# Forming the feed-forward weights inside the last attention output product, and a different split of the mixer's element-wise work between VectorE, ScalarE and GpSimd

## The chip, the cores and the metric

One core of a Trainium2 chip runs one program. The metric is the device time of that core in microseconds, the median of several runs. The core has a matrix engine (TensorE, in the rows PE, with PEld for its weight loads), VectorE (DVE), ScalarE (ACT), GpSimd (POOL) and a queue engine (SyncE, SP) that issues nearly all transfers. Each engine works through its own instruction list in order; semaphores join them.

## The reference, cut to what matters

`x` has 8 sequences of 512 positions and 1024 features. Four layers follow each other, each with a residual and a layer norm in front:

```
x = x + attention(layernorm(x))          # per sequence
x = x + ffn(layernorm(x))                # kind 1 in the kernel
x = x + mixer(layernorm(x))              # kind 2; mixes over the 8 sequences ("l") per position
x = x + ffn(layernorm(x))                # kind 3, the same weights as kind 1
ffn(x):   base = x @ W_base.T + b_base
          decoded_e = (x @ enc.T) @ (coefs_e * mask_e).T      # rank 40, three experts e
          return base + 0.5 * sum_e real_inverse_fourier(decoded_e)
mixer(x): x + up(xmid + gated two-layer state-space block(gelu(down(x))))
```

Everything in `ffn` behind `x` is linear, so the kernel forms one 1024 x 1024 weight `W = W_base.T + 0.5 * enc.T @ basis` with `basis = (sum of masked coefs).T @ inverse transform`. In the mixer each position's 8 x 8 causal weights over `l` are laid out as 128 x 128 matrices `cb`: entries ahead of a position, behind it, and ones on the diagonal.

## The kernel before, in words

**Attention program.** Tokens are handled in 8 sequences (`BATCH`) of 8 head groups each, one group per step `M` of a hand-written pipeline. The output product of a sequence comes in two runs of four token tiles (`output(b, run)`): each tile is 8 chunks of three float32r products (high x high, low x high, high x low), 24 matmuls of 512 columns, and VectorE adds it to the residual (`add_residual`, L718) before SyncE stores it in the DRAM array `x1` (L372). Products of float32 operands that are split into a float32r high part and a remainder stand for full precision throughout.

**Weights of the feed-forward layer.** The class `Setup` (`early`) holds buffers that lie in the same place in both programs. When the last AV product is done, SyncE loads the coefficients, masks, four pairs of rows of the inverse transform (`dft_pairs`), `enc` and the first two pairs of rows of `W_base` (L82 to L88). VectorE forms the masked sum (`mix_coefs`, L101 to L106). Behind the last output run TensorE computes `basis` in full float32, 16 products of 512 columns (L114); VectorE copies it to SBUF (L124); the program ends, and SyncE first waits for all of `x1`.

**Mixer program.** Work goes in 8 blocks of four token tiles; a tile is 16 positions of all 8 sequences, loaded by one transfer of 512 KB. The list `ORDER` is the hand-written order of stages for one turn of the loop, and each engine runs its part of each stage in that order. A stage belongs to an event `(kind, tile)`: `moments` (VectorE statistics L1329, L1331; GpSimd's inverse root L1177, L1179), `norm` (VectorE L1339), `turn` (8 TensorE transposes L1559, ScalarE's high part L1246, VectorE's low part L1346, GpSimd's `post`), `gemm` (24 matmuls per half L1564 to L1566), `add` (L1354). `down`, `h_...`, `up` are the mixer's own stages; `h_mix` (L1680) is the product with the 128 x 128 matrices.

Before the first turn stands a `head`: `weights`, then norm and turn of tiles (1,0) and (1,1). In `weights` TensorE forms the 8 row blocks of `enc.T @ basis` in full float32 (L1711, 16 products), VectorE adds each to `W_base` (L1516), ScalarE rounds the sum to float32r (L1303), VectorE forms the remainder (L1504). SyncE in the meantime issues the first two x tiles (L1146), the down weights (L1154), 17 parameters (L1156) and 7 constants (L1159), waits for six of the remainders, and loads six more x tiles (L1146): some x tiles lie where rows of `W_base` were. `post` of the first tile waits for all 24 parameters and constants (`late_in`).

`post(e)` on GpSimd, for kind 1 and 3, adds the bias to the residual in four pieces (L1193). For kind 2 the residual is the normed input as well, so it first adds `xn` in four pieces (L1189), then the bias in four. GpSimd handles `post` of tile (2,3) ahead of the inverse root of (3,0), as the order has it, and `norm(e)` waits for `post(e-2)`.

`h_weight` builds `cb`: VectorE multiplies the product in PSUM by a mask for one side (L1423), by the mask for the other side (L1425), copies an edge of the identity (L1427), adds the sides (L1429) and adds the identity (L1431); then it forms the step weights (L1436 to L1446). `h_mix` multiplies both (L1455) and TensorE takes the result (L1680).

Of the kernel before, what the change touches and what calls it, by code (L numbers as in the profile page):

```python
# [5 lines left out]
P = 128  # L6
# [7 lines left out]
U8 = mybir.dt.uint8  # L14
PENDING = []
# [7 lines left out]
class Setup:  # L23
# [5 lines left out]
    DMA = 16  # L29

    def __init__(self, nc, ctx, w, c):
# [7 lines left out]
        self.tok = self.place("tok", [P, 3, self.TILES, 256])  # L39
        self.mixer = self.place("mixer", [P, self.TILES, 4, P])  # L40
        self.h_mid = self.place("h_mid", [P, 2, self.COLS])
        self.mask = self.place("mask", [P, self.CH, experts, rank], U8)
        self.wsum = self.place("wsum", [P, self.CH, rank])
        self.ident = self.place("ident", [P, P])
        self.experts = experts
# [3 lines left out]
        self.enc = self.mixer[0:rank, 2:4, :, :].rearrange("p a b c -> p (a b c)")  # L49
        self.basis = self.h_mid[0:rank, :, :].rearrange("p a b -> p (a b)")  # L50
# [9 lines left out]
        self.basis_part, self.basis_ready, self.basis_done = sem("basis_part"), sem("basis_ready"), sem("basis_done")  # L60
# [19 lines left out]
    def load(self, sp):  # L80
# [5 lines left out]
        sp.dma_start(self.enc, self.w["enc"]).then_inc(self.params_in, self.DMA)  # L86
        for k in range(2):
            sp.dma_start(self.base_pairs[k], self.rows(self.w["base_t"], k)).then_inc(self.base_in, self.DMA)  # L88

    def load_rest(self, sp):  # L90
        for k in range(2, self.CH // 2):
            if k < self.CH // 2 - 1:
                sp.wait_ge(self.basis_part, k + 1)
            else:
                sp.wait_ge(self.basis_ready, 2)
            sp.dma_start(self.base_pairs[k], self.rows(self.w["base_t"], k)).then_inc(self.pair_in[k], self.DMA)

    def mix_coefs(self, dve):
# [5 lines left out]
        for n in range(2, self.experts):  # L104
            dve.wait_ge(self.wsum_step, n)
            nc.vector.tensor_tensor(wsum[:, :, :], wsum[:, :, :], coef[:, :, n, :], ALU.add).then_inc(self.wsum_step, 1)  # L106

    def basis_product(self, pe, banks):
        pe.wait_ge(self.wsum_step, self.experts)
        for n in range(self.CH):  # L110
            if n % 2 == 0:
                pe.wait_ge(self.pair_in[n // 2], self.DMA)
            for h in range(2):
                mm = self.nc.tensor.matmul(banks[0:self.RANK, h, :], self.wsum[:, n, :], self.dft(n)[:, h * self.COLS:(h + 1) * self.COLS],  # L114
                                           start=(n == 0), stop=(n == self.CH - 1))
                if n == self.CH - 1:
                    mm.then_inc(self.basis_ready, 1)
                elif n % 2 and h:
                    mm.then_inc(self.basis_part, 1)
        pe.wait_ge(self.params_in, 2 * self.DMA)  # L120

    def basis_out(self, dve, banks):
        dve.wait_ge(self.basis_ready, 2)
# [1716 lines left out]
```

## Time and profile before

| | us |
|---|---|
| median of 3 runs | 2946.47 (2938.45 to 2946.77) |
| the profiled execution's own time | 2937.39 |
| its span, first to last instruction | 2935.6 |
| TensorE busy | 2706.6 (92%) |
| VectorE busy | 1676.3 (57%) |
| ScalarE busy | 1151.1 (39%) |
| GpSimd busy | 947.0 (32%) |

A row of a timeline has the start and length of an instruction (or of several equal ones), its engine, line, and what it writes and reads; in brackets how long the engine stood idle ahead of it, and what ended that. Times in the trace are microseconds from the span's start. The attention part ends and the mixer part begins between 1640 and 1700 us; below this stretch is called the seam. A turn of the mixer's loop takes about 147 us, and there are 8.

### The profile page before, as it was taken

The page shows a single profiled execution, that of the slowest core. Times are in us where ns is not written, and L with a number is a line of the kernel's source. Part 1 is how long each engine was busy: PE and PEld are TensorE (multiplying, and loading weights), DVE is VectorE, ACT ScalarE, POOL GpSimd, SP SyncE. Part 2 cuts the span into 40 slices and gives each one's busy share as a digit, 9 for nine tenths or more (in the row PEclk, how much of TensorE's full clock was granted, in tenths as well). Part 3 has the DMA queues.
Part 4 walks back from the last instruction along what each step waited for, and adds up shares of the span by engine and source line. Part 5 has one row for each costly group of instructions (what it writes and reads, how often), then busy time and mean ns, then how long its engine had stood idle before and what let it go on. Part 6 is the DMA issues. An engine that isn't in the chain of part 4 may idle for free. (4 is left out here: it accounts for less than half of the span.)

```text
span 2935.6 us, 41188 instructions
## 1 busy us (share of the span) xinstructions
PE 2706.6 (92%) x14784; PEld 1961.1 (67%) x14784; DVE 1676.3 (57%) x4305; ACT 1151.1 (39%) x2509; POOL 947.0 (32%) x1460
## 2 busy tenths in 40 slices
PE   5888999999999999999999987999999999999988
PEld 3555666657566676575665566777777777777766
DVE  3563564663745646636444346666666666666653
ACT  3763464562644645626455013222222222222220
POOL 2333122221231122212313044444444444444412
PEclk8999999999999999999999888999999999999989
DMA  5764554454536455544455410010101010101001
GB/s 159 209 169 151 176 125 143 126 115 145 126 91 172 124 140 130 113 150 120 107 146 172 145 43 1 7 52 7 52 6 53 6 53 5 54 5 54 5 26 29
DMA packets 103628, 272.24 MB, mean 93 GB/s; under 512 B 12122, under 2 KB 23514, under 8 KB 101122
## 3 DMA queue, kind: packets, MB, share of 16 engines
q1 hardware_dynamic: 102706, 269.55, 34.0%
q8 instruction: 118, 1.93, 0.3%
q14 instruction: 84, 0.69, 0.1%
q10 hardware_dynamic: 720, 0.07, 0.0%
HBM read 168.40 MB, written 50.33 MB: 75 GB/s over the span
## 5 line engine op out<-in xcount | busy, mean ns | idle before, releaser
L668 DVE CUSTOM_DVE_ANT_0 ps_attn<-ps_attn,later_keys 128x512 f32<-128x512 f32 (+3 forms) x1024 | 488.1, 508 | 392.8 <-PE ps_attn L841 392.3
L474 POOL TENSOR_SCALAR_AFFINE_SELECT pt<-pt 128x512 f32<-128x512 f32 x256 | 163.4, 649 | 868.1 <-ACT pt L561 868.1
L1564 PE MATMUL ps_mixer<-m_w_hi,m_xt_hi 128*128 128x512 f32 x1024 | 418.2, 408 | 1.6 <-DVE m_xt_lo L1346 1.6
L561 ACT ACTIVATE pt<-ps_attn 128x512 f32<-128x512 f32 (+1 forms) x704 | 380.4, 558 | 82.8 <-PE ps_attn L868 75.8
L1566 PE MATMUL ps_mixer<-m_w_lo,m_xt_hi 128*128 128x512 f32 x1024 | 400.6, 391 | 0.0
L1565 PE MATMUL ps_mixer<-m_w_hi,m_xt_lo 128*128 128x512 f32 x1024 | 400.4, 391 | 0.0
L576 ACT ACTIVATE ps_attn<-ps_attn,top 128x512 f32<-128x512 f32 (+1 forms) x512 | 311.6, 609 | 214.7 <-DVE top L668 214.0
L841 PE MATMUL ps_attn<-k_stack,q_stack 96*128 96x512 f32 (+3 forms) x1024 | 304.0, 348 | 42.8 <-ACT ps_attn L576 17.5
L868 PE MATMUL ps_attn<-q_stack,k_stack 97*128 97x512 f32 (+1 forms) x704 | 298.1, 426 | 30.3 <-DMA q_stack<-top_rows 18.9
L1246 ACT CAST m_xt_hi<-ps_mixer 128x512 fp32r<-128x512 f32 x192 | 103.6, 589 | 506.0 <-PE ps_mixer L1559 505.7
L841 PEld LDWEIGHTS ps_attn<-k_stack,q_stack 96*128 96x128 f32 x1024 | 182.8, 194 | 105.4 <-ACT ps_attn L576 64.6
L1564 PEld LDWEIGHTS ps_mixer<-m_w_hi,m_xt_hi 128*128 128x128 f32 x1024 | 193.4, 189 | 60.6 <-issue 16.1
L1346 DVE TENSOR_TENSOR m_xt_lo<-ps_mixer,m_xt_hi 128x512 fp32r<-128x512 f32 x192 | 123.8, 686 | 184.3 <-ACT m_xt_hi L1246 184.3
L1566 PEld LDWEIGHTS ps_mixer<-m_w_lo,m_xt_hi 128*128 128x128 f32 x1024 | 193.0, 188 | 41.8
L1565 PEld LDWEIGHTS ps_mixer<-m_w_hi,m_xt_lo 128*128 128x128 f32 x1024 | 193.6, 189 | 40.2 <-issue 3.9
L771 PE MATMUL ps_attn<-xn_hi,wq_hi 128*128 128x512 f32 x512 | 212.5, 415 | 6.0 <-DVE xn_lo L655 6.0
L718 DVE TENSOR_TENSOR xr<-ps_attn,xr 128x512 f32<-128x512 f32 x64 | 44.3, 692 | 289.9 <-PE ps_attn L773 289.9
L868 PEld LDWEIGHTS ps_attn<-q_stack,k_stack 97*128 97x128 f32 x704 | 133.5, 190 | 110.9 <-ACT pt L561 42.5
L772 PE MATMUL ps_attn<-xn_hi,wq_lo 128*128 128x512 f32 x512 | 205.1, 401 | 0.0
L1193 POOL TENSOR_TENSOR m_xs<-m_xs,m_p_base_b 128x256 f32<-128x256 f32 x256 | 182.9, 746 | 65.2 <-DVE m_xn L1339 58.8
L773 PE MATMUL ps_attn<-xn_lo,wq_hi 128*128 128x512 f32 x512 | 202.7, 396 | 0.0
L875 PE MATMUL ps_attn<-pt,v_sb 128*32 128x512 f32 (+3 forms) x2048 | 201.6, 467 | 1.0 <-DVE att L692 0.4
(216 smaller groups left out, 4915.7 us busy)
## 6 DMA issues: line engine op xcount, KB each, us to landing
xr<-in_a_x SPq DMA_DIRECT2D x64, 512.0 KB, 6.6
q_stack<-q_hi SPq DMA_DIRECT2D x128, 256.0 KB, 5.6
wq_hi<-wq_split SPq DMA_DIRECT2D x56, 512.0 KB, 3.9
wq_lo<-wq_split SPq DMA_DIRECT2D x56, 512.0 KB, 4.9
q_stack<-q_lo SPq DMA_DIRECT2D x64, 256.0 KB, 6.8
wo_hi<-wo_split SPq DMA_DIRECT2D x8, 2048.0 KB, 8.1
wo_lo<-wo_split SPq DMA_DIRECT2D x8, 2048.0 KB, 13.3
x<-xr SPq DMA_DIRECT2D x32, 512.0 KB, 2.8
```

Of the source, the lines that this page charges most:

```text
L561: nc.scalar.activation(pt[k][:, heads[0]:heads[0] + len(heads), :].rearrange("p j t -> p (j t)"), ps[:, ST0 + n % 2, 0:width * len(heads)] ...
L576: nc.scalar.activation(bank, bank, ACT.Exp, scale=-1.0, bias=top[:, j * TILES + i:j * TILES + i + 1].bitcast(F32), accum_out=den[:, i - (T ...
L668: mm = nc.vector.tensor_tensor_reduce(part, part, later_keys[:, T - width:T], 1.0, NO_SCORE, ALU.add, ALU.min, top[:, j * TILES + i:j * TI ...
L771: nc.tensor.matmul(out, a_hi, b_hi, start=first, stop=False)
L772: nc.tensor.matmul(out, a_lo, b_hi, start=False, stop=False)
L773: return nc.tensor.matmul(out, a_hi, b_lo, start=False, stop=last)
L841: mm = nc.tensor.matmul(bank[:, m * width:(m + 1) * width], q_stack[0:KROWS, G % 3, j, i * P:(i + 1) * P], k_stack[0:KROWS, b % 2, 0:width ...
L868: nc.tensor.matmul(ps[:, ST0 + n % 2, 0:width * len(heads)].rearrange("p (j t) -> p j t", t=width), k_stack[:, b % 2, k * P:(k + 1) * P], ...
L875: mm = nc.tensor.matmul(ps[j * HEAD:(j + 1) * HEAD, bank, k * P:end], side, pt[k][:, j, 0:end - k * P], start=(k == 0), stop=(k == TILES - ...
L1564: nc.tensor.matmul(out, a_hi, b_hi, start=first, stop=False)
L1565: nc.tensor.matmul(out, a_lo, b_hi, start=False, stop=False)
L1566: return nc.tensor.matmul(out, a_hi, b_lo, start=False, stop=last)
```

## The change

1. **Within the last output run.** The basis product runs ahead of the run instead of behind it. Its stationary operand is widened: the 40 ranks are placed in 120 columns (`PLACES`), so that one float32r product over 120 rows sums high x high, low x high and high x low. ScalarE rounds `enc` and `basis`, GpSimd and VectorE form the low rows. Between the run's tiles TensorE computes the row blocks of the delta (8 blocks of two float32r products), VectorE adds them to `W_base`, ScalarE rounds; VectorE forms the remainders of blocks 0 to 2, the statistics of the first two x tiles and the norm of the first, and only then adds the last output tile. SyncE loads these two x tiles as soon as their rows of `x1` are stored.
2. **Start of the mixer program.** Remainders of blocks 3, 4, 5 are formed by VectorE, 6 and 7 by GpSimd, the down weights' parts by ScalarE and VectorE behind the second turn. SyncE's order is: base bias, down weights, x tiles (1,0) and (1,1) of the second block, the other 16 parameters and 7 constants, then x tiles (0,2), (0,3), (1,2), (1,3). `post` of the first tile waits for the base bias alone.
3. **Kind 2's residual.** ScalarE computes `x * (1 + inv_std) - mean * inv_std` in one instruction behind its high parts of that tile; GpSimd forms the two factors (three small instructions behind the inverse root), and `post` has only the four bias adds, which wait for ScalarE. `norm(e)` no longer waits for `post(e-2)`.
4. **cb.** Set to the identity once; per use, two predicated copies put the two sides where the masks are not zero. The five instructions and the buffer `cb_fw` go.

The core of the diff:

```diff
+    STACK = 120
+    PLACES = ((0, 0, 40), (40, 0, 24), (64, 0, 40), (104, 24, 16))
+    LOW_FIRST = 3
+    DELTA = (2, 5, 0)
...
+    def delta_product(self, pe, banks, chunks):
+        for n in chunks:
+            if n == 0:
+                pe.wait_ge(self.enc_rows_in, 2 * self.DMA)
+                pe.wait_ge(self.basis_done, 2)
+            if n >= 3:
+                pe.wait_ge(self.sum_done, n - 2)
+            for h in range(2):
+                self.nc.tensor.matmul(banks[:, self.DELTA[n % 3] + h, :], self.enc[:, n * P:(n + 1) * P],
+                                      self.basis[:, h * self.COLS:(h + 1) * self.COLS], start=True,
+                                      stop=True).then_inc(self.delta_ready, 1)
+    def add_delta(self, dve, banks, chunks):
+        for n in chunks:
...
+            self.nc.vector.scalar_tensor_tensor(base, banks[:, bank:bank + 2, :], self.SCALING, base, ALU.mult,
+                                                ALU.add).then_inc(self.sum_done, 1)
+    def load_first(self, sp, x1):
+        sp.wait_ge(self.x1_out[0], x1.shape[0] * self.DMA)
+        sp.wait_ge(self.x1_out[2], x1.shape[0] * self.DMA)
...
             def _(sp):      # attention
+                    if M == NG:
+                        early.load_enc_rows(sp)
+                    if M == NG + 1:
+                        early.load_rest(sp)
+                        store_tile(BATCH - 1, 2, 0)
+                        early.load_first(sp, x1)
+                        store_tile(BATCH - 1, 2, 1)
+                        store(BATCH - 1, 3)
-                for n in range(TILES):
-                    sp.wait_ge(x1_out[n], BATCH * DMA)
...
             def _(dve):     # attention
+                    if M == NG + 1:
+                        early.basis_low(dve, ps)
+                        for t, chunks in ((0, (0, 1, 2)), (1, (3, 4, 5)), (2, (6, 7))):
+                            add_residual(BATCH - 1, 1, (t,))
+                            early.add_delta(dve, ps, chunks)
...
+                        for n in range(early.LOW_FIRST):
+                            early.weight_low(dve, early.w_lo_first[:, n, :], n)
+                        early.first_moments(dve, 0)
+                        early.first_moments(dve, 1)
+                        early.first_norm(dve, 0)
+                        add_residual(BATCH - 1, 1, (3,))
...
             def _(pe):      # attention
+                    if M == NG + 1:
+                        early.basis_product(pe, ps)
+                        output(BATCH - 1, 1, {0: (0, 1, 2), 1: (3, 4, 5), 2: (6, 7)})
-                early.basis_product(pe, ps)
...
             def _(sp):      # mixer
-                load(0, 0)
-                load(0, 1)
+                for n in range(3):
+                    sp.wait_ge(early.x1_out[n], (L + n // 2) * DMA)
+                sp.dma_start(par["base_b"][:], w["base_b"]).then_inc(early.params_in, DMA)
                 sp.dma_start(down_raw, w["down_t"]).then_inc(down_in, DMA)
+                sp.wait_ge(early.x1_out[3], L * DMA)
+                load(1, 0)
+                load(1, 1)
                 for n in names:
...
-                for i, t, n in ((0, 2, 6), (0, 3, 6), (1, 0, 6), (1, 1, 6), (1, 2, 6), (1, 3, 6)):
+                sp.wait_ge(wlo_done, 6)
+                for i, t in ((0, 2), (0, 3), (1, 2), (1, 3)):
                     load(i, t)
...
             def _(pool):    # mixer, inv_sqrt(e) of kind 2
+                        nc.gpsimd.tensor_scalar(res_gain[:, n % 2:n % 2 + 1], inv_std[:, s], 1.0, None, ALU.add).then_inc(res_scale, 1)
+                        nc.gpsimd.tensor_scalar(res_mean[:, n % 2:n % 2 + 1], mean_var[:, e % 2, 0:1], -1.0, None, ALU.mult).then_inc(res_scale, 1)
...
+                        nc.gpsimd.tensor_tensor(res_shift[:, n % 2:n % 2 + 1], res_mean[:, n % 2:n % 2 + 1], inv_std[:, s],
+                                                ALU.mult).then_inc(res_scale, 1)
                 def post(e):
...
                     if kind == 2:
-                        for cols in pieces:
-                            nc.gpsimd.tensor_tensor(stream[:, cols], stream[:, cols], xn[:, e % 2, cols], ALU.add).then_inc(up_bias, 1)
-                        pool.wait_ge(up_bias, PIECES * (kind2.index(e) + 1))
+                        pool.wait_ge(res_done, kind2.index(e) + 1)
...
+                for n in (6, 7):
+                    pool.wait_ge(whi_done, n + 1)
+                    nc.gpsimd.tensor_tensor(w_lo(n), base(n), w_hi[:, n, :].bitcast(F32), ALU.subtract).then_inc(wlo_last_done, 1)
...
             def _(act):     # mixer
+                def add_normed(e):
+                    n, stream = kind2.index(e), stream_of(e)
+                    act.wait_ge(xn_done, e + 1)
+                    act.wait_ge(res_scale, 3 * (n + 1))
+                    nc.scalar.activation(stream, stream, ACT.Identity, bias=res_shift[:, n % 2:n % 2 + 1],
+                                         scale=res_gain[:, n % 2:n % 2 + 1]).then_inc(res_done, 1)
...
             def _(dve):     # mixer
                 def norm(e):
                     if e >= 2:
                         dve.wait_ge(xt_ready, 2 * (e - 1))
-                        dve.wait_ge(post_done, PIECES * (e - 1))
...
                 def h_weight(q):
-                    nc.vector.tensor_tensor(cb_fw[:, :, PB:P], cb_ps[:, :, 0:cut],
-                                            con["before"][:, None, PB:P].to_broadcast([P, TILES, cut]), ALU.mult).then_inc(cb_step, 1)
...
-                    nc.vector.tensor_tensor(cb[:, :, 0:cut], cb[:, :, 0:cut],
-                                            con["ident"][:, None, 0:cut].to_broadcast([P, TILES, cut]), ALU.add).then_inc(cb_done, 1)
+                    nc.vector.copy_predicated(cb[:, :, PB:P], con["before"][:, None, PB:P].to_broadcast([P, TILES, cut]).bitcast(U32),
+                                              cb_ps[:, :, 0:cut]).then_inc(cb_done, 1)
+                    dve.wait_ge(cb_done, 2 * q + 1)
+                    nc.vector.copy_predicated(cb[:, :, 0:cut], con["after"][:, None, 0:cut].to_broadcast([P, TILES, cut]).bitcast(U32),
+                                              cb_ps[:, :, PB:P]).then_inc(cb_done, 1)
```

## Rows read from the trace of the kernel before

**Rows 1.** Busy time by engine in one turn: stretch, length, busy per engine, clock, DMA.

```profile
2031.00:2178.00 147.00, 142.88 (x775) 113.33 (x774) 96.99 (x196) 37.42 (x61) 66.78 (x120) 1.00 0.11 29
```

**Rows 2.** Waits of PE, 1740 to 2890 us: total, times, longest.

```profile
PE ps_mixer L1680 <- DVE m_mixer L1455: 17.5, 8, 6.0
...
PE ps_mixer L1559 <- DVE m_xn L1339: 13.7, 9, 2.2
```

**Rows 3.** Timeline of PE within two turns: start, length, line, idle before.

```profile
1939.53 2.37 PE L1680 MATMUL ps_mixer<-m_mixer,m_tok 128*64 128x128 f32 x32 [1.22 <-DVE m_mixer L1455]
...
1995.32 1.03 PE L1559 MATMUL ps_mixer<-m_ident,m_xn 128*128 128x128 f32 x8
...
2030.63 1.09 PE L1559 MATMUL ps_mixer<-m_ident,m_xn 128*128 128x128 f32 x8 [1.74 <-DVE m_xn L1339]
```

**Rows 4.** Timeline of PE at the seam: first basis products, first and third transposes.

```profile
1645.61 3.63 PE L114 MATMUL ps_attn<-m_xn,m_wsum 128*40 128x512 f32 x8
...
1697.08 1.94 PE L1559 MATMUL ps_mixer<-m_ident,m_xn 128*128 128x128 f32 x8 [8.01 <-DVE m_xt_lo L1346]
...
1705.92 1.03 PE L1559 MATMUL ps_mixer<-m_ident,m_xn 128*128 128x128 f32 x8
```

**Rows 5.** Line L1711, the delta products: min, median, max ns; first and last start.

```profile
L1711 PE MATMUL ps_mixer<-m_h_mid,m_mixer x32: 589/1057/1057, 1662.1 to 1686.1; 40*128 40x512 f32 x32
```

**Rows 6.** Busy time by engine in two stretches of the first product (columns of Rows 1).

```profile
1696.00:1700.00 4.00, 2.92 (x11) 2.76 (x12) 2.54 (x5) 1.18 (x2) 0.00 (x0) 0.50 0.51 134
1700.00:1704.00 4.00, 4.00 (x14) 3.13 (x14) 2.58 (x5) 0.00 (x0) 1.04 (x3) 0.71 0.52 137
```

**Rows 7.** Timeline of VectorE at the seam.

```profile
1629.47 0.69 DVE L718 TENSOR_TENSOR xr<-ps_attn,xr 128x512 f32<-128x512 f32 x1 [3.95 <-PE ps_attn L773]
1634.91 0.69 DVE L718 TENSOR_TENSOR xr<-ps_attn,xr 128x512 f32<-128x512 f32 x1 [4.75 <-PE ps_attn L773]
...
1659.58 1.22 DVE L124 COPY m_h_mid<-ps_attn 40x1024 f32<-40x1024 f32 x1 [12.74 <-PE ps_attn L114]
...
1666.81 1.23 DVE L1516 SCALAR_TENSOR_TENSOR m_xs<-ps_mixer,m_xs 128x1024 f32<-128x1024 f32 x1 [1.38 <-PE ps_mixer L1711]
```

**Rows 8.** Timeline of SyncE's issues at the seam.

```profile
1661.46 1.38 SPq L1146 DMA_DIRECT2D m_xs<-x  x2
...
1672.24 4.47 SPq L1156 DMA_DIRECT2D m_p_gate<-in_m_gate  x1
...
1682.99 0.43 SPq L1159 DMA_DIRECT2D m_c_same<-in_c_same  x1
...
1686.81 4.05 SPq L1146 DMA_DIRECT2D m_xs<-x  x6
```

**Rows 9.** Landing of all transfers into the x tiles' buffer, 1600 to 1720 us.

```profile
DMA to landing us min/median/max: 5.3/12.9/16.3
```

**Rows 10.** Chain of work, from a tile's statistics to its norm.

```profile
1726.31 1.30 DVE m_stats L1329 x2
...
1728.89 0.82 DVE m_xn L1339
```

**Rows 11.** Timeline of VectorE, first and sixth instruction of `h_weight`.

```profile
1934.28 0.61 DVE L1423 TENSOR_TENSOR m_cb_fw<-ps_mixer,m_c_before 128x448 f32<-128x448 f32 x1
...
1936.83 0.17 DVE L1436 TENSOR_TENSOR m_d_term<-ps_mixer,m_p_d_row 128x16 f32<-128x16 f32 x1
```

**Rows 12.** Timeline of GpSimd at a turn's end, first and last of 16 adds.

```profile
2017.08 3.24 POOL L1189 TENSOR_TENSOR m_xs<-m_xs,m_xn 128x256 f32<-128x256 f32 x4
...
2026.03 2.80 POOL L1193 TENSOR_TENSOR m_xs<-m_xs,m_p_up_b 128x256 f32<-128x256 f32 x4
```

**Rows 13.** Timeline of ScalarE: a scaled and biased copy, and two high parts.

```profile
1894.77 1.64 ACT L1268 ACTIVATE m_feat<-ps_mixer,m_p_conv_b,m_p_conv_w 128x512 f32<-128x512 f32 x2 [1.12 <-PE ps_mixer L1625]
...
1987.80 1.07 ACT L1246 CAST m_xt_hi<-ps_mixer 128x512 fp32r<-128x512 f32 x2 [3.27 <-PE ps_mixer L1559]
...
2019.69 1.07 ACT L1246 CAST m_xt_hi<-ps_mixer 128x512 fp32r<-128x512 f32 x2
```

More of the change, by code:

```diff
@@ new lines, in weights_high, with weight_low @@
+    def weights_high(self, act):
+        for n in range(self.CH):
+            act.wait_ge(self.sum_done, n + 1)
+            self.nc.scalar.copy(self.w_hi[:, n, :], self.base(n)).then_inc(self.whi_done, 1)
+    def weight_low(self, dve, place, n):
+        dve.wait_ge(self.whi_done, n + 1)
+        self.nc.vector.tensor_tensor(place, self.base(n), self.w_hi[:, n, :].bitcast(F32), ALU.subtract).then_inc(self.wlo_done, 1)
+    def load_first(self, sp, x1):
+        sp.wait_ge(self.x1_out[0], x1.shape[0] * self.DMA)
+        sp.wait_ge(self.x1_out[2], x1.shape[0] * self.DMA)
+        tiles = x1.rearrange("l (i t b) d -> i t l b d", t=self.TILES, b=P // x1.shape[0])
+        for t in range(2):
+            sp.dma_start(self.xs[:, 0, t, :], tiles[0, t]).then_inc(self.x_in[t], self.DMA)
@@ L533, in _ @@
                         add_bias(M // GROUPS - 1, 3)
+                early.enc_low(pool)
+                for t in range(2):
+                    early.first_inv_sqrt(pool, neg_half[:, :], t)
+                pool.wait_ge(early.std_done, 4)
             @block.scalar
@@ L710, in kv_in, with add_residual @@
                                           ).then_inc(v_done, 1)
-                def add_residual(b, run):
-                    for t in range(TILES):
+                def add_residual(b, run, tiles=range(TILES)):
+                    for t in tiles:
                         n = 2 * run + t // 2
@@ L1300, in weights @@
                 def weights():
-                    for n in range(CH):
-                        act.wait_ge(sum_done, n + 1)
-                        nc.scalar.copy(w_hi[:, n, :], base(n)).then_inc(whi_done, 1)
                     act.wait_ge(down_in, DMA)
@@ L1532, in _ @@
                     if name == "weights":
-                        weights()
+                        early.weight_low(dve, w_lo(3), 3)
                     elif name == "moments" and event(i, what) >= 2:
                         moments(event(i, what))
-                    elif name == "norm" and event(i, what) >= 2:
+                    elif name == "norm" and event(i, what) >= 1:
                         norm(event(i, what))
```

275 lines of the change are left out of this document (159 added, 116 removed).

## The prediction

> **What bounds the kernel now.** I read the busy time by stretch first, then who waits for whom on TensorE, then the timelines of the places where it waits. In a turn of the mixer TensorE is busy for 142.9 of 147 us at the full clock, VectorE for 97, ScalarE for 37, GpSimd for 67 [rows 1]. So the loop is bound by TensorE, and what an edit can gain there is at most the 4.1 us that TensorE stands idle. Two waits make most of that: `h_mix` stands 1.22 us for the first mixer matrix from VectorE, and the transposes of tile (3,0) stand 1.74 us for their norm [rows 3]. Over the whole mixer the first kind sums to 17.5 us in 8 waits (two long ones, in the first and the last turn, where TensorE has nothing else to do), the second to 13.7 us in 9 [rows 2].
>
> The other loss is the seam. TensorE ends the last output tile at 1645.6, computes the basis until 1659.6 [rows 4, 7], then the delta at half speed, 32 passes of which the median takes 1.06 us, into 1687 [rows 5], stands 8.0 us, and begins its first steady work, the transposes of the second tile, at 1697.1; the third tile's follow at 1705.9 [rows 4]. SyncE issues transfers from 1661.5 to 1683.4, and only then asks for the third x tile, at 1686.8 [rows 8]. From the third tile on, TensorE runs without a break for 30 us, so what reaches that point earlier is gained, and nothing else of the seam is.
>
> **The seam, step by step.** The threshold for all that follows: differences under 0.3% (9 us) can't be told from no change here.
>
> TensorE in the last run: the basis stays at 13.97 us [rows 4, 7], since the moving operand keeps its 512 columns and more stationary columns don't lengthen it. It is moved ahead of the run, which hides the masked sum. The delta becomes 16 products at the rate of the output tile (24 in 5.44 us [rows 7], so 0.23 each): 3.6 us. TensorE ends at 1659.6 + 3.6 = 1663.
>
> VectorE becomes last there. Its last delta is ready one tile earlier, at about 1657.8. Then it has two sums at 1.2 us and three remainders of the same size [rows 7], 6.1 us; statistics of two tiles, 1.5 each with their aggregate, a norm of 0.8 [rows 10] and the postponed output add of 0.7 [rows 7]: together 10.6, to 1668.4. The program's end costs what it cost before (1660.8 to 1661.5 [rows 7, 8]), so the mixer begins at about 1669, 7.6 us later than now. This wait is new: queued behind the sums on VectorE are the last add, the last store and the block's end, and everyone waits for it.
>
> In the mixer program the first tile is normed already. Transposes, high and low part, two remainders, the second norm and its transposes take VectorE and TensorE some 7 us; the first half product runs from 1676 to 1683, at half clock for its first part. GpSimd's two remainders are needed for its last quarter only, and even at twice the 2.8 us of a bias add of that size [rows 12] they are there.
>
> Then TensorE needs the third x tile, and SyncE is late with it. Ahead of it in its queue stand the base bias, the down weights, the wait for the last store of `x1`, two x tiles and 23 parameters and constants, from about 1672 on. Bounds for the 23: the 12 issues between the gate's and the last took 6.3 us, so 0.52 each and 12 us together; or all at the mean of the 25 before (1662.8 to 1683.4, 0.82 each, the gate's alone 4.47 [rows 8]) and 19 us. I take 16, nearer the slow end, since two x tiles stand ahead of them in the queue as before, and the rows of `W_base` no longer do. That gives 1688; the tile lands 5.3 us behind its issue at best [rows 9], and its norm is done 3.4 us later [rows 10]: transposes at about 1697.3 instead of 1705.9, 8.6 us earlier. But TensorE has stood for 14 us then. After its 8.0 us of idleness before, its clock was 0.50 and then 0.71 of full over two stretches of 4 us [rows 4, 6]; that lost 0.5 x 2.9 + 0.29 x 4 = 2.6 us, which now falls behind the third tile. **Gain at the seam: 6 us; with the bounds 3 to 10.**
>
> **The turns.** *cb.* Six VectorE instructions start within 1934.28 to 1936.83 [rows 11]: the five that go hold 2.55 us. A predicated copy doesn't occur in the trace; the nearest row is the product with a mask of the same 448 columns from PSUM, 0.61. Two, the second behind the first's completion, are 1.25; if each is twice the row, 2.45 and nothing is won; if each is 0.4, 0.8. I take the row: 1.3 us won, more than the 1.22 of the steady wait. It is gained in full in six turns (6 x 1.22 = 7.3) and as 1.3 in the first and the last (2.6). Behind it TensorE is the bound.
>
> *Kind 2's residual at the end of a turn.* Now GpSimd's 16 adds for (2,2) and (2,3) run from 2017.1 to 2028.8 [rows 12], then comes the inverse root for (3,0), its norm, and TensorE, 1.74 us late [rows 3]. Of these, eight adds go. In exchange the others wait for ScalarE: high part of (2,2) until 2020.8 [rows 13], then the scaled copy. Its nearest rows are two scaled and biased copies of half the size, 1.64 us, and two plain ones, 1.07 [rows 13]; I take 1.25, for one instruction of the full size has its fixed part once. So the eight adds run from 2022.0 to 2027.6, 1.2 us earlier than now; about 1.1 are left behind the added small instructions. Over seven ends of a turn: 7.7 us. At 1.64 it is 0.7 each, at 1.07 1.3: 5 to 9. That ScalarE then delays the high part of (2,3) by 0.2 us is within this.
>
> Here a rule speaks against the edit. The Trainium skill ("ScalarE: Activation LUTs", section "Rules for kernel authors") gives multiplications and additions to VectorE, as the faster engine. A norm of that size takes 0.8 us on VectorE [rows 10] against my 1.25, and by the rule the chain could be 0.4 us shorter and the sum 3 us better. ScalarE is idle for three quarters of a turn [rows 1], though, so no engine that is bound pays for it.
>
> *The other tiles of kind 2.* The bias adds of (2,1) now start behind ScalarE: high part until 1988.9, copy 1990.1, adds 1992.9, inverse root and norm of (1,3) at most 2.1 us [rows 10], 1995.0. TensorE takes that tile at 1995.3 [rows 3, 13]: hidden, with 0.3 us to spare. In the first turn TensorE has less between, and I charge 0.9 us. GpSimd's three small instructions stand behind the inverse root that VectorE waits for, and cost nothing as long as GpSimd is idle for half a turn [rows 1].
>
> **The sum.** 6.0 + 7.3 + 2.6 + 7.7 - 0.9 = 22.7 us. The profiled execution took 2937.4, which gives 2914.7. The median before is 2946.5, 9.1 above it, and one run of three lies where the profiled one does; I put the forecast between, at **2919**.
>
> **Rivals.**
> 1. *SyncE's queue is short.* With 12 us for the 23 issues the third tile comes 4 us earlier: 2915, and less if TensorE's clock stays up. For it: no `W_base` in the queue. Against: the x tiles. 0.15.
> 2. *The queue is as slow as before.* The third tile then comes at 1700, the seam gives 3 us: 2922. For it: one transfer of 0.5 KB held the queue 4.5 us [rows 8]. 0.15. The Trainium skill ("DMA: Bandwidth & Descriptors", section "Rules for kernel authors") says of transfers under 64 KB that one pays mostly overhead, and most of the 23 are that small; the trace's slow issue agrees.
> 3. *Predicated copies cost as much as what they replace.* 9.9 us of the sum go: 2929. 0.1.
> 4. *ScalarE's chain becomes the bound (slower).* Each us that the scaled copy takes beyond 1.25 is lost at (3,0) and, beyond 0.3, at (1,3), in each of 7 turns. The rest of the sum is 15; from 2.5 us more on, the kernel is slower by over 0.3%, and with 3 more it loses 7 x (1.9 + 2.7) - 15 = 17: 2959. Only a copy of 4 us does that; the rows say 1.1 to 1.6. 0.05.
> 5. *The change doesn't shorten the seam or the waits*: the weights' work is done sooner, but the postponed output add and the late tile eat it, and another input is late for `h_mix`. 2940. Against it: the waits' releasers in the rows are the very instructions that go. 0.1.
>
> **Numbers.** The forecast has 0.45. The range takes in cases 1 to 3 with their bounds: low, seam 10, residual 9, cb 11 and the faster runs, 2906, and some 6 below it for a clock that stays up; high, the slower runs less 10, 2937. Faster by over 0.3%: the forecast, cases 1 to 3, less a little: 0.83; within 0.3%: 0.11; slower: 0.06.
>
> **What would show it.** Right: basis and delta of the last run at full clock, no L1711 behind; VectorE as the last engine at the attention's end; an idle stretch of some 14 us on TensorE ahead of the third transposes, ended by the x tile's statistics; SyncE's last parameter near 1688; the wait of L1680 gone in steady turns, that of L1559 down to 0.6 us; turns of 144.7 us. Wrong: predicated copies of over a microsecond each, a scaled copy over 1.6 us, a wait of (1,3) or (2,1) in each turn, or a third tile that is there when TensorE asks for it.

## The result, and the profile after

The changed kernel took 2921.23 us (median of 4 runs, 2918.71 to 2924.96), the kernel before 2946.62 beside it (4 runs, 2938.45 to 2947.54): a ratio of 0.9921, with a 95% interval of 0.9903 to 0.9938. In a second comparison, on another chip, it was 2927.12 (6 runs) against 2940.53 (11 runs): 0.9951, 0.9937 to 0.9966. So it is faster, by 13 to 25 us.

Part of what varies from one execution to the next stands before any changed instruction. SyncE's first issue for the new weights (the rank coefficients) comes behind the whole attention; its place in the timeline of the kernel before, and then of the changed kernel:

```profile
1600.63 0.34 SPq L82 DMA_DIRECT2D m_mixer<-in_m_coefs  x1
```

```profile
1604.67 0.34 SPq L104 DMA_DIRECT2D m_mixer<-in_m_coefs  x1
```

In the twelve profiled executions of this study that issue lies between 1597.3 and 1614.4 us, with the same attention work ahead of it. All readings below are therefore counted **from the coefficients**: span less this issue. That is 1335.0 us before (2935.6 - 1600.63) and 1314.8 after (2919.5 - 1604.67): a gain of **20.1 us** by this measure. It has a spread of its own: a second profile of the changed kernel gives 1317.2, and two kernels below that should be alike (`align`, `pad512`) differ by 3.4, so differences of some 3 us in it are not read. Why the two comparisons differ is not shown: the second profile is the fastest of its six runs (2921.26), and the slower ones have none.

PE's timeline at the seam and at the ends of turns, changed kernel:

```profile
1672.64 1.94 PE L1692 MATMUL ps_mixer<-m_ident,m_xn 128*128 128x128 f32 x8 [5.11 <-PEq L439]
...
1681.63 1.97 PE L1692 MATMUL ps_mixer<-m_ident,m_xn 128*128 128x128 f32 x8 [7.05 <-DVE m_xn L1492]
...
1702.27 1.97 PE L1692 MATMUL ps_mixer<-m_ident,m_xn 128*128 128x128 f32 x8 [11.98 <-DVE m_xn L1492]
...
1729.50 1.09 PE L1692 MATMUL ps_mixer<-m_ident,m_xn 128*128 128x128 f32 x8 [1.16 <-DVE m_xn L1492]
1737.22 1.09 PE L1692 MATMUL ps_mixer<-m_ident,m_xn 128*128 128x128 f32 x8 [1.09 <-DVE m_xn L1492]
...
1878.23 1.09 PE L1692 MATMUL ps_mixer<-m_ident,m_xn 128*128 128x128 f32 x8 [0.21 <-DVE m_xn L1492]
...
2023.64 1.09 PE L1692 MATMUL ps_mixer<-m_ident,m_xn 128*128 128x128 f32 x8 [0.58 <-DVE m_xn L1492]
...
2750.78 1.09 PE L1692 MATMUL ps_mixer<-m_ident,m_xn 128*128 128x128 f32 x8 [0.57 <-DVE m_xn L1492]
```

The third transposes come 97.6 us behind the coefficients, against 105.3 before [rows 4]: 7.7 earlier. The rows at 1729.50 and 1737.22 are the tiles (2,1) and (1,3) of the first turn; the kernel before has no wait for (2,1) there and 0.97 us for (1,3). The wait at the end of a turn is 0.58 us instead of 1.74 [rows 3]. Five turns, from 2023.64 to 2750.78, make 145.43 each; before, from 2030.63 to 2765.45, 146.96.

Waits of PE from 1700 us on (total, times, longest), changed kernel:

```profile
PE ps_mixer L1692 <- DVE m_xn L1492: 17.9, 10, 12.0
...
PE ps_mixer L1815 <- DVE m_mixer L1605: 7.5, 2, 4.7
```

The six steady waits for the mixer matrix are gone (8 waits and 17.5 us in [rows 2]); the first and the last turn's are left, shorter.

VectorE and SyncE at the seam, changed kernel (one fence each):

```profile
1664.12 3.48 DVE L195 TENSOR_TENSOR m_w_lo_first<-m_xs,m_w_hi 128x1024 fp32r<-128x1024 f32 x3
...
1671.03 0.68 DVE L830 TENSOR_TENSOR xr<-ps_attn,xr 128x512 f32<-128x512 f32 x1
...
1675.84 4.60 DVE L195 TENSOR_TENSOR m_w_lo_last<-m_xs,m_w_hi 128x1024 fp32r<-128x1024 f32 x2
...
1698.81 1.29 DVE L1483 BATCH_NORM_STATS2 m_stats<-m_xs 128x6 f32<-128x512 f32 x2 [12.13 <-DMA m_xs<-x]
```

```profile
1676.57 0.46 SPq L1292 DMA_DIRECT2D m_p_up_b<-in_m_up_b  x1
...
1691.91 0.43 SPq L1295 DMA_DIRECT2D m_c_same<-in_c_same  x1
1692.39 2.61 SPq L1277 DMA_DIRECT2D m_xs<-x  x4
```

VectorE is the last engine of the attention, and its last output add stands behind remainders and statistics; the mixer starts at 1672.6. Then the third x tile is late: SyncE asks for it at 1692.4, behind 23 parameters and constants that took 15.8 us; its statistics start 6.4 us later, and TensorE has stood for 12.

The new instructions (groups of the changed kernel: busy us, mean ns):

```profile
L1578 DVE COPY_PREDICATED m_cb<-m_c_before,ps_mixer 128x448 f32<-128x448 uint32 x16 | 10.5, 657 | 8.1 <-PE ps_mixer L1798 8.1
L1581 DVE COPY_PREDICATED m_cb<-m_c_after,ps_mixer 128x448 f32<-128x448 uint32 x16 | 10.7, 667 | 0.6
L1401 ACT ACTIVATE m_xs<-m_xs,m_res_shift,m_res_gain 128x1024 f32<-128x1024 f32 x32 | 40.1, 1253 | 0.2
L176 PE MATMUL ps_attn<-m_basis,m_enc_stack 120*128 120x512 f32 x16 | 4.2, 393 | 0.0
```

**What doesn't fit.** TensorE's idle time in a turn fell by 2.5 us, the turn by 1.53. Busy time by engine in one turn, changed kernel (columns of [rows 1]):

```profile
2023.64:2169.07 145.43, 143.78 (x772) 113.33 (x772) 95.04 (x190) 41.98 (x65) 59.15 (x115) 1.00 0.11 30
```

TensorE is busy for 143.8 us where it was 142.9 [rows 1], with the same instructions and the clock at 1.00. The loss is in the products with the FFN weights. The second and the last of 48 such products without a break, kernel before, then changed:

```profile
2043.79 0.39 PE L1565 MATMUL ps_mixer<-m_w_hi,m_xt_lo 128*128 128x512 f32 x1
...
2054.24 0.39 PE L1566 MATMUL ps_mixer<-m_w_lo,m_xt_hi 128*128 128x512 f32 x1
```

```profile
2036.85 0.39 PE L1698 MATMUL ps_mixer<-m_w_hi,m_xt_lo 128*128 128x512 f32 x1
...
2047.46 0.39 PE L1699 MATMUL ps_mixer<-m_w_lo_last,m_xt_hi 128*128 128x512 f32 x1
```

46 steps take 10.45 us before (0.2272 each) and 10.61 after (0.2307). The other stretches of the turn (22 or 70 steps) show 0.227 to 0.229 before and 0.230 to 0.231 after; over all of them a step is 1.3% longer. What moved for these products is the place of their operands in a partition: `w_hi` now stands in the region that exists during the attention. Before, `xt_hi` began 73728 bytes behind `w_hi` (18 x 4096); now 83072 (20 x 4096 + 1152).

### The profile page after: what moved, and what is told of

Same layout as the page of the kernel before. It is cut to its first block, busy times and chain, and to the rows that moved or that the text cites. A ratio compares the mean times of both kernels' runs of the same rounds, so it can differ in the third digit from the quotient of the medians.

```text
span 2919.5 us, 41088 instructions
## 1 busy us (share of the span) xinstructions
PE 2692.6 (92%) x14768; PEld 1958.6 (67%) x14768; DVE 1667.5 (57%) x4261; ACT 1189.4 (41%) x2544; POOL 895.7 (31%) x1430
## 4 chain that ended last, share of the span: by engine, by line
PE 71%; DVE 11%; issue 5%; DMA 4%; ACT 4%; POOL 2%; SPq 1%; DVEq 0%; ACTq 0%; POOLq 0%
PE ps_attn L895 8%; PE ps_mixer L1697 8%; PE ps_attn L896 8%; PE ps_attn L897 8%; PE ps_mixer L1698 8%; PE ps_mixer L1699 8%; PE ps_attn L999 4%; PE ps_attn L965 4%; DVE ps_attn L780 3%; PE ps_attn L992 3%; DMA q_stack<-q_lo 2%; PE ps_mixer L1692 2%; DVE att L790 2%; ACT ps_attn L684 2%; POOL m_xs L1339 1%
## 5 line engine op out<-in xcount | busy, mean ns | idle before, releaser
L1699 PE MATMUL ps_mixer<-m_w_lo_last,m_xt_hi 128*128 128x512 f32 x640 | 249.8, 390 | 0.0
L895 PE MATMUL ps_attn<-wo_hi,at_hi 128*128 128x512 f32 x480 | 187.5, 391 | 1.4 <-DVE xr L830 1.3
```

The costliest lines, as they stand in the source:

```text
L895: nc.tensor.matmul(out, a_hi, b_hi, start=first, stop=False)
L1699: return nc.tensor.matmul(out, a_hi, b_lo, start=False, stop=last)
```

## The experiments

Each is the changed kernel with one edit, but for `old_seam`, which is the kernel before with two, `pad512` and `pad128`, which add to `align`, and `early_free` and `gpsimd_first`, which join several. The code below is shortened: arguments and semaphores are left out. All were compared with the kernel before on their chip:

| kernel | median (runs) | ratio to before, 95% | from the coefficients | a turn |
|---|---|---|---|---|
| before | 2946.62 (4) | 1 | 1335.0 | 146.97 |
| changed | 2921.23 (4) | 0.9921 (0.9903 to 0.9938) | 1314.8 | 145.43 |
| changed, run again | 2927.12 (6) | 0.9951 (0.9937 to 0.9966) | 1317.2 | 145.45 |
| align | 2917.08 (6) | 0.9903 (0.9885 to 0.9922) | 1312.8 | 144.60 |
| pad512 | 2916.21 (1) | not given | 1309.4 | 144.59 |
| pad128 | 2939.01 (1) | not given | 1324.8 | 146.01 |
| x_first | 2915.54 (4) | 0.9895 (0.9881 to 0.9910) | 1306.9 | 145.42 |
| old_seam | 2925.87 (6) | 0.9933 (0.9917 to 0.9950) | 1316.2 | 144.45 |
| old_cb | 2938.39 (12) | 0.9973 (0.9961 to 0.9985) | 1328.6 | 146.72 |
| old_res | 2937.38 (12) | 0.9988 (0.9977 to 0.9998) | 1327.8 | 146.62 |
| early_free | 2908.95 (5) | 0.9886 (0.9870 to 0.9902) | 1299.5 | 144.60 |
| gpsimd_first | 2906.93 (5) | 0.9873 (0.9855 to 0.9891) | 1292.6 | 144.60 |

**align: the weights back at whole distances.**

```diff
+        self.place("gap", [P, 288])
         self.w_hi = self.place("w_hi", [P, self.CH, D], F32R)
-        par = {n: ... for n in ("base_b", "up_b", "wz_t", "wdt_t", "conv_w")}
+        par = {n: ... for n in ("base_b", "up_b")}
```

> The changed kernel, with w_hi and the first three chunks of w_lo moved up by 1152 bytes of a partition and three small parameters moved behind xt_lo: again, as in the kernel before, every weight tensor stands a whole number of 4096 bytes from the transposed inputs (now 83072 bytes, 20 x 4096 + 1152, between w_hi and xt_hi). No instruction is added, removed or reordered. In the changed kernel each of the 384 weight products of a turn takes 0.231 us where it took 0.228. Theory A: that is the place of the tensors. Then a product takes 0.228 again, a turn 144.5 us instead of 145.4, and the whole 8 x 1.0 = 8 us less than the changed kernel: about 2913. Theory B: it is the traffic of another engine (ScalarE's scaled copy, GpSimd), or drift: turns stay at 145.4 and the time at 2921. Theory C: the place of xt alone matters, which does not move here: also 2921.

```profile
2017.52:2162.12 144.60, 142.90 (x772) 113.28 (x772) 95.07 (x190) 41.99 (x65) 59.09 (x115) 1.00 0.11 30
```

This turn has TensorE busy for 142.9 us again, and lasts 144.60. Theory A; B and C are out, since no other engine's work and not the place of `xt_hi` changed. From the coefficients only 2.0 us of some 6.6 (8 x 0.83) are seen. In the first turn the granted clock was 0.94 and 0.93 over two stretches of 20 us (from 1714.87) in which the changed kernel's was 1.00, which costs up to 2.6 us by itself, and the last turn was 0.8 us longer too. `pad512` below, with products as quick and without that stretch, shows 5.4 us.

**pad512 and pad128: how exact the distance must be.** Both are `align` with free bytes ahead of `xt_hi`.

```diff
+        sb("gap_xt", [P, 128])     # pad512; [P, 32] in pad128
         xt_hi, xt_lo = sb("xt_hi", [P, CH, 3, P], F32R), sb("xt_lo", [P, CH, 3, P], F32R)
```

> The kernel with the restored distances, with 512 bytes of a partition left free ahead of xt_hi, so that the distance of the weights to the transposed inputs is 512 bytes over a whole multiple of 4096. Theory A: only the place within 512 bytes counts: a weight product takes 0.228 us, a turn 144.6. Theory B: the distance counts within a larger period (1024 to 4096): 0.231 us, 145.4.

> The kernel with the restored distances, with 128 bytes of a partition left free ahead of xt_hi: nothing but the places of xt_hi, xt_lo and what stands behind them changes. Theory A: the distance of weights to inputs within 512 bytes is what slowed the products: they take 0.231 us again and a turn 145.4. Theory B: the distance is innocent (the three small parameters that moved, or the place of the weights by themselves, did it): 0.228 us and 144.6.

The products of `w_hi` with `xt_lo` in pad512, then in pad128 (busy us, mean ns):

```profile
L1700 PE MATMUL ps_mixer<-m_w_hi,m_xt_lo 128*128 128x512 f32 x1024 | 399.7, 390 | 0.0
```

```profile
L1700 PE MATMUL ps_mixer<-m_w_hi,m_xt_lo 128*128 128x512 f32 x1024 | 405.3, 396 | 0.0
```

Turns of 144.59 and 146.01 us. Theory A in both: 512 bytes more do no harm, 128 do, and more than in the changed kernel (145.4, which theory A had said for `pad128`), where the five chunks of `w_lo_last` stood at a whole distance (28672 bytes) by chance. Their products show it, in the changed kernel and then in pad128:

```profile
L1699 PE MATMUL ps_mixer<-m_w_lo_last,m_xt_hi 128*128 128x512 f32 x640 | 249.8, 390 | 0.0
```

```profile
L1701 PE MATMUL ps_mixer<-m_w_lo_last,m_xt_hi 128*128 128x512 f32 x640 | 252.6, 395 | 0.0
```

The weights stand in the same place in `align` and in the slow `pad128`, and `xt_hi` stands in the same place in `align` and in the slow changed kernel: neither place by itself makes the difference. One run each; turns within a run differ by less than 0.1 us.

**old_seam: the edits of the turns alone.** The kernel before, with the predicated copies and ScalarE's residual of the diff above; all else stays.

> The kernel before, with the two edits of the mixer's turns alone (predicated copies for cb, the residual of the down branch by ScalarE) and without the moved weights: the delta is still made in the mixer, from the 40 rank rows at full precision, and w_hi, w_lo and the inputs keep their places. Theory A (my sum): the turns give 7.3 + 2.6 + 7.7 - 0.9 = 16.7 of the 22.7 us, so 2930 against 2946.6 for the kernel before, and the moved weights 6 to 9 us; and as the weights have not moved, a turn takes 144.5 us, not the 145.4 of the changed kernel. Theory B: the slower products of the changed kernel come from the two edits of the turns: then a turn takes 145.4 here too, and the time is 2937. Theory C: the seam gives nothing: this kernel runs like the changed one, 2921, or faster by the 8 us of its quicker products.

```profile
2032.70:2177.15 144.45, 142.73 (x773) 113.28 (x773) 95.09 (x190) 41.99 (x65) 59.03 (x115) 1.00 0.11 30
```

A turn of 144.45: the two edits alone give the 144.7 that the prediction wanted, and the slower products are not theirs (theory B is out). From the coefficients they gain 18.8 us, 16.7 expected. The whole change gains 20.1: the moved weights bring their 7.3 us at the third transposes (104.9 here, 97.6 after) and lose nearly as much again in the products. Theory C saw that end, though not by its cause. With the products as quick as here, what the moved weights are worth in all is 3.4 us by `align` and 6.8 by `pad512`; the prediction said 6.0.

**old_cb: the masked correlation by five instructions.**

```diff
-  nc.vector.copy_predicated(cb[:, :, PB:P], before, cb_ps[:, :, 0:cut])
-  nc.vector.copy_predicated(cb[:, :, 0:cut], after, cb_ps[:, :, PB:P])
+  tensor_tensor(cb_fw[:, :, PB:P], cb_ps[:, :, 0:cut], before, ALU.mult)
+  tensor_tensor(cb[:, :, 0:cut], cb_ps[:, :, PB:P], after, ALU.mult)
+  tensor_copy(cb[:, :, cut:P], ident); tensor_tensor(cb, cb, cb_fw, ALU.add)
+  tensor_tensor(cb[:, :, 0:cut], cb[:, :, 0:cut], ident, ALU.add)
```

> The changed kernel with the masked correlation put together by five instructions again (two masked products, a copy, two adds) in place of two predicated copies. Theory A: VectorE's chain ahead of the mixer matrix is 1.2 us longer, and it is what ends last there: the wait of TensorE for the mixer matrix is back in each of the six steady turns with 1.1 to 1.2 us, and is 1.2 longer in the first and the last: 8 x 1.2 = 9.6 us, 2931. Theory B: another input of the mixer matrix (the decay weights) comes hardly earlier, and the predicated copies won less than half of that: 2922 to 2926.

```profile
PE ps_mixer L1823 <- DVE m_mixer L1613: 17.0, 8, 6.0
```

The waits are back, 17.0 us against 7.5, and a turn is 1.29 us longer. Theory A. From the coefficients it is 13.8 us behind the changed kernel, 11.4 behind its second profile; most of what goes beyond 9.5 lies in the first and the last turn, where the granted clock differs from run to run.

**old_res: the residual on GpSimd again.**

```diff
-  pool.wait_ge(res_done, kind2.index(e) + 1)
+  for cols in pieces:
+      tensor_tensor(stream[:, cols], stream[:, cols], xn[:, e % 2, cols], ALU.add)
-  nc.scalar.activation(stream, stream, ACT.Identity, bias=res_shift, scale=res_gain)
+  dve.wait_ge(post_done, PIECES * (e - 1))     # in norm(e)
```

> The changed kernel with the residual of the down branch on GpSimd again (eight adds more per pair of tiles, none by ScalarE). Theory A: the transposes of tile (3,0) stand at the end of each turn for 1.7 us again instead of 0.58: 7 x 1.15 = 8 us, a turn of 146.6 us instead of 145.4, and a median near 2929. Theory B: the edit takes more from GpSimd than that one wait shows, and the tiles (2,1) and (1,3) become late as well: over 12 us, above 2933. Theory C: ScalarE's share was won or lost elsewhere and the wait at (3,0) was only moved: under 3 us, 2921 to 2924.

PE's timeline at the ends of the first two turns, and the clock (last but two) behind the first:

```profile
1876.80 1.48 PE L1675 MATMUL ps_mixer<-m_ident,m_xn 128*128 128x128 f32 x8 [2.22 <-DVE m_xn L1475]
...
2025.00 1.09 PE L1675 MATMUL ps_mixer<-m_ident,m_xn 128*128 128x128 f32 x8 [1.74 <-DVE m_xn L1475]
```

```profile
1878.00:1880.00 2.00, 2.00 (x5) 0.97 (x4) 1.75 (x3) 0.67 (x2) 1.61 (x3) 0.50 0.00 0
```

Theory A in the turns (146.62, waits of 1.74), but the loss from the coefficients is 13.0 us (10.6 against the second profile), not 8. That is theory B's size without its mechanism: (2,1) has no wait here. Five turns lose 6.0. Another 3.6 lie about the end of the first turn, where the wait is 2.22 instead of 0.21 and the granted clock falls to 0.50 behind it, the lower of its two levels (1.2 of 2.4 GHz). The kernel before has both as well (2.23 us at 1882.11, a clock of 0.50 from 1884 to 1886); the changed kernel has neither. The last 3.6 lie in the last turn: from 60 us behind the last such transposes the clock was 0.79, 0.59 and 0.77 over three stretches of 20 us, against 0.80, 0.69 and 0.83 in the changed kernel. Whether the edit has a part in that is not shown.

**x_first: SyncE's queue in another order.**

```diff
+                for dst, src in late[:10]: sp.dma_start(dst[:], src)
                 sp.wait_ge(wlo_done, 6)
+                load(0, 2)
+                load(0, 3)
+                for dst, src in late[10:]: sp.dma_start(dst[:], src)
+                for t in range(TILES): load(1, t)
```

> The changed kernel, with SyncE's queue in another order at the start of the mixer: ten parameters, then the wait for six remainders, then the x tiles (0,2) and (0,3), then the other parameters and constants, and block 1's four tiles last. In the changed kernel the tile (0,2) is asked for at 1692.4, although its place is free at 1680.4, and TensorE stands 12 us for it until 1702.3. Theory A (the queue's order is the seam's limit): the tile is asked for at 1680.5 to 1681, lands 5 to 7 us later, and the third transposes start near 1691, 11 us earlier; all after it moves: 2910 to 2912. Theory B (the seam is held by something else, a slow landing beside the parameters or TensorE at half speed): 4 to 6 us, 2915 to 2917. Theory C (the parameters, 4 us later now, are missed by the first turn): what is won is lost near 1730, and the time is 2919 to 2923.

SyncE's issue and PE's third transposes:

```profile
1685.07 1.22 SPq L1277 DMA_DIRECT2D m_xs<-x  x2
```

```profile
1695.91 1.10 PE L1691 MATMUL ps_mixer<-m_ident,m_xn 128*128 128x128 f32 x8 [1.80 <-DVE m_xn L1491]
```

The transposes come 19.1 us behind the mixer's start, not 29.6, at full clock; from the coefficients they come 10.2 us earlier (87.4 against 97.6), and 7.9 are won in all, with 2.0 lost in the last turn. Theory A for the place; the time (2915.5) reads like B, with the attention 4 us later than in the changed kernel's profile. No parameter is missed.

**early_free: chunks 4 and 5 first, and the weights at whole distances.**

```diff
+    LOW_ORDER = (4, 5, 0, 1, 2, 3, 6, 7)
     store_tile(BATCH - 1, 2, 1)
+    sp.wait_ge(self.wlo_done, 2); load x(0,2), x(0,3)
...
     x_low(0)
-    weight_low(4); weight_low(5); norm(1)
+    norm(1); weight_low(2); weight_low(3)
```

> The changed kernel with the weights at whole distances of 4096 bytes again, and with the first three remainders made for chunks 4, 5 and 0 instead of 0, 1 and 2. Chunks 4 and 5 hold the place of the x tiles (0,2) and (0,3): SyncE can ask for these within the last output run, ahead of the last store. In the mixer the norm of tile (1,1) comes before the remainders 2 and 3. Times are counted from the start of the first transposes of the mixer, since the attention's part drifts by some 8 us from run to run. Theory A: the second transposes start 4 us after the first instead of 9.0, the third 14 us after them instead of 29.6 (19.1 with the reordered queue), without a wait for an x tile; with the 8 x 0.83 us of the quicker products this is 22 us better than the changed kernel: 2899 to 2903. Theory B: VectorE and GpSimd slow each other at the start of the mixer (two remainders took 4.60 us there, 1.2 each alone), a weight is late for the first product, and the third transposes come 19 us after the first, as with the reordered queue: 2904 to 2909. Theory C: the two loads delay the last store of x1 and the end of the attention block by as much as they win: 2911 to 2915.

PE, then GpSimd:

```profile
1674.15 1.97 PE L1697 MATMUL ps_mixer<-m_ident,m_xn 128*128 128x128 f32 x8 [2.12 <-DVE m_xn L1497]
...
1686.72 1.97 PE L1697 MATMUL ps_mixer<-m_ident,m_xn 128*128 128x128 f32 x8 [3.54 <-DVE m_xn L1497]
```

```profile
1677.66 7.26 POOL L1344 TENSOR_TENSOR m_xs<-m_xs,m_p_base_b 128x256 f32<-128x256 f32 x8 [1.35 <-DMA m_p_base_b<-in_m_base_b]
1684.89 0.22 POOL L1317 TENSOR_SCALAR m_var_eps<-m_mean_var 128x1 f32<-128x1 f32 x1
```

The second transposes come 4.1 us behind the first (1670.09), as in theory A; the third 16.6, between A and B, and no x tile is waited for. What is late next is an inverse root that stands behind eight bias adds in GpSimd's queue. From the coefficients 15.3 us are won, where theory A said 22; the median (2908.95) is at the slow end of B.

**gpsimd_first: that inverse root ahead of the second four adds**, and the down weights' remainder behind the norm.

```diff
                     elif name == "turn":
+                        if event(i, what) == 1: inv_sqrt(2)
                         post(event(i, what))
```

> The changed kernel once more, unaltered, beside the kernel below on one chip. If the attention's drift is chance, its coefficients are asked for somewhere between 1597 and 1613 us, the third transposes of the mixer come 97.6 us behind that and a steady turn takes 145.4 us, as in its first profile; its median may then lie up to 8 us from 2921, and its ratio to the kernel before between 0.991 and 0.995. If the drift belongs to the program, the coefficients are asked for within 1 us of 1604.7 and the median is 2921 again.

> The kernel that frees chunks 4 and 5 early, with two more changes of order: GpSimd makes the inverse root of tile (1,2) ahead of the base bias of tile (1,1), and VectorE makes the remainder of the down weights behind the norm of (1,2) instead of ahead of its statistics. There the third transposes stood 3.54 us, for an inverse root that waited 1.9 us behind GpSimd's eight bias adds. Theory A (that queue is what ends last): the wait falls to under 0.5 us, the third transposes come 13.1 us after the first instead of 16.6, and the time is 3 us better: 2904 to 2907. Theory B (TensorE's clock gives it back): the transposes come earlier, but the first turn starts no sooner, 98 us later instead of 95.6 to 98.1, since TensorE is at half speed for longer: 2907 to 2910.

```profile
1682.61 1.94 PE L1699 MATMUL ps_mixer<-m_ident,m_xn 128*128 128x128 f32 x8 [5.12 <-PEq L444]
1686.67 1.97 PE L1699 MATMUL ps_mixer<-m_ident,m_xn 128*128 128x128 f32 x8 [2.12 <-DVE m_xn L1499]
...
1696.48 1.09 PE L1699 MATMUL ps_mixer<-m_ident,m_xn 128*128 128x128 f32 x8 [0.74 <-DVE m_xn L1499]
```

The third transposes come 13.9 us behind the first (13.1 said, 16.6 in `early_free`), with a wait of 0.74 us (under 0.5 said), and the first sums with `ones` 94.0 behind those (at 1790.47, against 98.1 in `early_free`): nearer to theory A, and B is out. The 4 us between the third transposes and those sums are not the edit's by any run; the clock differs there. It has the lowest median, 2906.9 against 2927.1 and 2940.5 on one chip, but its ratio (0.9873) can't be told from that of `early_free` (0.9886); from the coefficients it takes 22 to 25 us less than the changed kernel. The changed kernel, run again, has its coefficients at 1602.3, 2.4 us from the first time: the drift is not the program's, as the first theory says, with the turns at 145.45; its third transposes came 98.8 behind them (97.6 expected), its ratio reached 0.9951.

## Why the prediction was right, and where it was not

The forecast was 2919 us, with a sum of 22.7; measured were 2921.2 and 2927.1, and 20.1 us from the coefficients (17.8 in the second profile). That 2919 came within 2.3 us of the first median is in part luck: the sum was 2.6 to 4.9 too large, and the 4.3 us put on top of it covered that.

- **The seam's steps held.** The mixer starts 7.1 us later from the coefficients (68.0 against 60.8, where [rows 8] begin); 7.6 were said. The basis kept its 592 ns for each product with 120 columns in place of 40. VectorE is the last engine, the 23 issues took 15.8 us (16 taken; rivals 1 and 2 had 12 and 19), the tile's statistics began 6.4 us behind its issue (5.3 taken for the landing), TensorE stood for 12.0 (14), and the third transposes came 7.7 earlier (8.6 said, though the terms give 1688 + 5.3 + 3.4 = 1696.7, not 1697.3, and so 9.2). The clock then was 0.50 up to 1704 and 0.69 up to 1708, some 2.1 us by the prediction's own reckoning (2.6 charged).
- **The predicated copies** took 657 and 667 ns (0.61 us taken). The waits fell by 10.0 us in all; 9.9 were said. Rival 3 is out.
- **The scaled copy** took 1253 ns (1.25 taken), the wait at (3,0) fell to 0.58 (0.6); rival 4 is out, and in steady turns neither (2,1) nor (1,3) waits. The Trainium skill ("ScalarE: Activation LUTs", section "What ACT_TABLE_LOAD costs") gives 186 ns + 0.833 ns per element and 93 ns for each per-partition operand, by which an estimate for this copy is 1225 ns: the trace agrees within 3%. That VectorE would have done better here, no run shows.
- **The failed step: "Behind it TensorE is the bound", with its 142.9 us taken as fixed.** The change moves `w_hi` and the first three chunks of `w_lo`, and with them 304 of the 384 products of a turn stand 128 bytes off; over all 384 a step became 1.3% longer. A turn gave 1.53 us, not 2.3. By `align` that is 0.83 us in each turn, some 6 to 7 us in all (5.4 by `pad512`), nearly all that the seam brought. On the timeline, the 20.1 us are 7.7 up to the third transposes, 0.2 from there to the end of the first turn, 10.8 in the six turns behind it and 1.4 in the rest; the prediction's terms, placed likewise, are 8.6, -1.1, 13.9 and 1.3, so the six turns fell short.
- **The first turn: the charge came, and a gain was overlooked.** "In the first turn TensorE has less between, and I charge 0.9 us" held in size, at (2,1) more than at (1,3): the waits there are 1.16 and 1.09 us, and with the residual on GpSimd (`old_res`) none and 0.94. But the end of that turn is where the residual's edit gained most: a wait of 2.2 us became 0.2, where 1.1 was said for each end, and the clock of 0.50 behind it went too.
- **The own run and the median.** The forecast was placed 4.3 us above the sum for a drift of the runs. The drift is real, and part of it stands in the attention; what in it varies was not looked into.

## What to carry to other kernels

Where a change moves an operand of TensorE, compare the start-to-start time of the same products in both traces before crediting or blaming anything else: a fixed bound is only fixed while its operands stay where they are. When an input is late at the start of a stage, read SyncE's queue from its issue backwards, and free the place of the first tile before those of the later ones. Count a difference of under 1% from an event behind the part that drifts, not from the start of the program.

## What the runs showed of the hardware

- The step of a float32r product of 128 x 512 depends on the distance within a partition between its two operands. At whole multiples of 512 bytes a turn took 144.5 to 144.6 us (`align`, `old_seam`, `pad512`; 0.2272 us for a step in the stretch shown of the kernel before). With 304 of 384 products 128 bytes off it took 145.4 (changed kernel, 0.2307), and 146.0 with all of them off (`pad128`). Other remainders than 128 were not tried, and the cause isn't known.
- A wait of TensorE of 2.2 us was followed by a granted clock of 0.50 at the end of the first turn, in the kernel before and in `old_res`; behind the 0.2 us of the changed kernel, and behind the 1.74 us at the ends of the later turns, the clock stayed at 1.00. The length of the wait alone does not decide it: early in the first turn TensorE stands 1.1 and then 1.6 us at the same place of the changed kernel (from 1736.1) and of `align` (from 1728.2); behind it the clock stayed at 1.00 in the first and was 0.57 over 4 us in the second.
- At the mixer's start two remainders took VectorE 4.60 us, while three took 3.48 within the output run; GpSimd was then forming its own two, and transfers were landing. The two are one of 1.32 us and one of 3.36. The slow one, and the remainder of GpSimd that was under way when it began:

```profile
1677.08 3.36 DVE L195 TENSOR_TENSOR m_w_lo_last<-m_xs,m_w_hi 128x1024 fp32r<-128x1024 f32 x1
```

```profile
1676.04 3.32 POOL L1376 TENSOR_TENSOR m_w_lo_last<-m_tok,m_w_hi 128x1024 fp32r<-128x1024 f32 x1
```

  VectorE's ends 1.08 us behind GpSimd's, about the time that it takes alone (1.22). So does the one of 1.32 us, which began 0.24 us before GpSimd's first ended, and so do the slow ones in `early_free` and `gpsimd_first`, where the order differs (3.38 us each). The remainder that VectorE began 0.18 us ahead of GpSimd's first took 1.23. The transfers are not what slowed it: their engines were busier then (a DMA share of 1.05, against 0.68 while the slow one stood), and in the kernel before, where GpSimd forms no remainders, five of VectorE's took 1.22 each at shares of 0.62 to 1.07. The Trainium skill ("GPSIMD Engine Reference", section "8. Key points") says that GpSimd shares its SBUF interfaces with VectorE and contends with VectorE's instructions of two SBUF inputs, which these are; the trace agrees.
